# One core, a kernel of linear attention and a feed-forward layer: the store of the second weight's scales and their reload become two steps of the DMA queue, and the order of all steps is drawn anew

## What is computed

```python
x = x + attn(layernorm(x))     # attn: own norm, q,k,v = xn @ W (16 heads of 64), chunks of 128 rows
    # per head and chunk:  G = K.T @ K + 1e-4 I;  W = solve(G, K.T @ V)
    # U = I[:, :8]; twice: U = qr(W @ U).Q;  Wr = U @ (U.T @ W)
    # S = 0.9 * S + Wr;  out = 0.125 * (Q @ S);  attn = x + concat(out) @ Wo
x = x + ffn(layernorm(x))
    # bw = mean(|w|, axis=1) * sign(w) for w1 (1024 x 256) and w2 (256 x 1024)
    # out = gelu(x @ bw1.T + b1) @ bw2.T + b2
```

## Time and profile before

| what | value |
|---|---|
| median of 3 runs | 826.64 us (826.21 to 831.26) |
| the profiled execution | 823.01 us |
| its span, first to last instruction | 821.2 us |
| PE busy, share of the span | 756.2 us, 92% |
| DVE busy, share | 558.9 us, 68% |
| ACT busy, share | 483.2 us, 59% |
| POOL busy, share | 79.4 us, 10% |

### The profile page before, as it was taken

One profiled execution on the slowest core, in us unless ns is written; L12 is line 12 of the kernel. 1 busy time (PEld: TensorE's weight loads), 2 busy tenths in 40 slices (PEclk: granted clock), 3 DMA queues, 4 the chain that ended last, 5 costly groups with the idle time before them and its releaser, 6 DMA issues.

```text
span 821.2 us, 28518 instructions
## 1 busy us (share of the span) xinstructions
PE 756.2 (92%) x12336; PEld 494.7 (60%) x12336; DVE 558.9 (68%) x1530; ACT 483.2 (59%) x1000; POOL 79.4 (10%) x60
## 2 busy tenths in 40 slices
...
GB/s 257 294 28 87 138 73 58 154 132 164 50 110 161 139 100 91 139 101 152 89 116 102 196 160 125 150 98 97 90 195 59 168 74 59 86 86 77 54 26 26
DMA packets 262766, 93.63 MB, mean 114 GB/s; under 512 B 225008, under 2 KB 255984, under 8 KB 261616
## 3 DMA queue, kind: packets, MB, share of 16 engines
...
## 4 chain that ended last, share of the span: by engine, by line
PE 49%; DVE 23%; DMA 8%; issue 8%; ACT 5%; SPq 4%; POOL 1%; DVEq 0%; ACTq 0%; POOLq 0%
PE ring L1120 13%; DVE outer L936 8%; PE wide L1160 7%; DVE ax L945 6%; PE tok L1327 6%; PE ring L1138 3%; PE ring L1315 3%; PE wide L1247 3%; PE tok L1297 2%; PE small L1278 2%; PE sum L1288 2%; DMA ax<-lead_d 2%; DMA ax<-comp_d 2%; PE small L1168 2%; DVE rd L928 1%
## 5 line engine op out<-in xcount | busy, mean ns | idle before, releaser
L1120 PE MATMUL ring<-wkv,xt 128*128 128x512 f32 x512 | 245.0, 620 | 9.0 <-ACT rest L697 8.8
L936 DVE SCALAR_TENSOR_TENSOR outer<-ax,rd 128x448 f32<-128x448 f32 (+15 forms) x368 | 186.1, 533 | 8.8
L945 DVE TENSOR_TENSOR ax<-ax,outer 128x448 f32<-128x448 f32 (+15 forms) x368 | 163.2, 470 | 4.4
L1120 PEld LDWEIGHTS ring<-wkv,xt 128*128 128x128 f32 x512 | 93.4, 194 | 107.5 <-issue 90.0
L1327 PE MATMUL tok<-s2t,wkv 128*128 128x256 f16 x512 | 63.9, 282 | 8.3 <-DVE wkv L1045 7.5
L681 ACT COPY vals<-ring 128x512 f32<-128x512 f32 x64 | 37.3, 586 | 56.0 <-PE ring L1120 55.8
L577 POOL TENSOR_TENSOR root<-rdc,pos_half 128x32 f32<-128x32 f32 x8 | 43.4, 5428 | 266.6 <-DVE rdc L953 266.6
L1045 DVE TENSOR_TENSOR wkv<-ht,wkv 128x512 f16<-128x512 f32 x64 | 42.9, 688 | 37.9 <-ACT wkv L842 37.7
L1315 PE MATMUL ring<-y,s1t 128*128 128x512 f16 x256 | 61.8, 380 | 1.3 <-ACT ht L835 1.3
L1327 PEld LDWEIGHTS tok<-s2t,wkv 128*128 128x128 f16 x512 | 50.1, 101 | 20.0 <-DVE wkv L1045 10.7
L835 ACT ACTIVATE ht<-ring,b1c,alpha 128x512 f32<-128x512 f32 x64 | 48.9, 778 | 20.2 <-PE ring L1315 17.0
...
## 6 DMA issues: line engine op xcount, KB each, us to landing
...
xf<-inv_d SPq DMA_DIRECT2D x128, 32.0 KB, 2.1
```

Source lines behind the costliest of these rows:

```text
L936: at = note(V.scalar_tensor_tensor(out=t, in0=a[:, k, r0:r1].unsqueeze(2).broadcast_to([P, rows, cols]), scalar=r, in1=a[:, k, r0:HALF + k ...
L945: ends.append(note(V.tensor_tensor(rest, rest, t, ALU.subtract)))
L1120: ins = mm(dst[:], xt[:, g % 2, t, P * k:P * (k + 1)], weight[:, t, BANK * j:BANK * (j + 1)], start=t == 0, stop=t == KT - 1)
```

## The change

The step `al` is cut in two: `a1` stores the scales (after DVE has made them), `al` waits for the store and loads them back. In SP_ORDER `al` stood before `gs:7`; now `la:0`, the load of the first pass's lanes, stands first, then `cs:1 a1 cs:2 al`. At the same time all five tables are drawn anew. The steps in them are the same, apart from `a1`, and each does what it did: the instructions, their shapes and their number are unchanged. All lines below L378 move down by 2 in the new file.

```diff
-            def spread_alpha():
+            def store_alpha():
                 sp.wait_ge(alpha_done, 2)
                 load(alpha2_d.rearrange("(t p) -> p t", p=P), alpha2[:], allow_slow_non_contiguous=True).then_inc(alpha_stored, 16)
+
+            def spread_alpha():
                 sp.wait_ge(alpha_stored, 16)
                 load(alpha2r[:], alpha2_d.rearrange("(a d) -> a d", a=1).broadcast_to([P, DM])).then_inc(alpha_loaded, 16)
...
 SP_ORDER = """
-x:0 x:1 c w:0.0 w:0.1 w:1.0 w:1.1 zs wq wo b1 ff b2 rs:0 xs:0 xs:1 rs:1 gs:0 gs:1 x:2 x:3 gs:2 gs:3 gs:4 gs:5
-cs:0 rs:2 gs:6 x:4 al gs:7 cs:1 la:0 cs:2 xs:2 cs:3 rs:3 x:5 gs:8 cs:4 gs:9 gs:10 cs:5 gs:11 cs:6 xs:3 cs:7 rs:4
...
+x:0 c w:0.0 w:0.1 x:1 w:1.0 w:1.1 zs wq wo b1 ff b2 rs:0 xs:0 rs:1 gs:0 gs:1 xs:1 cs:0 x:2 x:3 gs:2 gs:3 gs:4
+gs:5 rs:2 gs:6 gs:7 x:4 la:0 cs:1 a1 cs:2 al xs:2 cs:3 rs:3 x:5 gs:8 gs:9 cs:4 gs:10 gs:11 cs:5 cs:6 xs:3 cs:7
...
```

More of the change, by code:

```diff
@@ L70 @@
+H:7.5 H:7.6 H:7.7 O:7.0 O:7.1
 """
 ACT_ORDER = """
-own norm:0 XT:0.0 XT:0.1 XT:1.0 XT:1.1 norm:1 K:0.0 K:0.1 K:1.0 K:1.1 K:2.0 G:0 K:2.1 G:1 K:3.0 K:3.1 K:4.0
-K:4.1 mag:0 K:5.0 K:5.1 K:6.0 mag:1 K:6.1 K:7.0 G:2 G:3 K:7.1 mag:2 V:0.0 V:0.1 G:4 G:5 C:0 V:1.0 norm:2 G:6
-V:1.1 WQ:0 mag:3 G:7 V:2.0 C:1 V:2.1 WQ:1 WQ:2 C:2 V:3.0 V:3.1 XT:2.0 XT:2.1 C:3 norm:3 K:8.0 K:8.1 K:9.0 K:9.1
-V:4.0 K:10.0 V:4.1 G:8 K:10.1 C:4 G:9 K:11.0 V:5.0 K:11.1 V:5.1 G:10 C:5 V:6.0 G:11 V:6.1 WQ:3 S2:0 C:6 V:7.0
-V:7.1 XT:3.0 XT:3.1 C:7 norm:4 K:12.0 K:12.1 K:13.0 K:13.1 G:12 K:14.0 G:13 K:14.1 K:15.0 K:15.1 T:0 G:14 G:15
@@ L103 @@
-hi:6.2 AU:30 AU:31 H:6.3 hi:6.3 H:6.4 H:6.5 hi:6.4 hi:6.5 H:6.6 H:6.7 hi:6.6 hi:6.7 n3:7 X3:7.0 X3:7.1 H:7.0
-H:7.1 hi:7.0 hi:7.1 H:7.2 H:7.3 hi:7.2 hi:7.3 H:7.4 H:7.5 hi:7.4 hi:7.5 H:7.6 H:7.7 hi:7.6 hi:7.7
+own norm:0 XT:0.0 XT:0.1 K:0.0 norm:1 K:0.1 K:1.0 K:1.1 K:2.0 G:0 K:2.1 G:1 K:3.0 K:3.1 V:0.0 V:0.1 XT:1.0
+XT:1.1 C:0 mag:0 K:4.0 K:4.1 K:5.0 G:2 G:3 K:5.1 K:6.0 mag:1 K:6.1 K:7.0 G:4 G:5 K:7.1 V:1.0 norm:2 G:6 G:7
+V:1.1 mag:2 C:1 mag:3 V:2.0 V:2.1 WQ:0 WQ:1 C:2 V:3.0 V:3.1 XT:2.0 XT:2.1 C:3 norm:3 K:8.0 K:8.1 K:9.0 K:9.1
@@ new lines @@
+K:10.0 V:4.0 G:8 K:10.1 V:4.1 G:9 K:11.0 C:4 K:11.1 V:5.0 V:5.1 G:10 G:11 V:6.0 C:5 V:6.1 WQ:2 WQ:3 C:6 V:7.0
+V:7.1 XT:3.0 XT:3.1 C:7 norm:4 K:12.0 K:12.1 K:13.0 K:13.1 G:12 K:14.0 G:13 K:14.1 K:15.0 T:0 K:15.1 G:14 G:15
+V:8.0 V:8.1 S2:0 C:8 V:9.0 V:9.1 S2:1 VS:0 C:9 ST:0 V:10.0 V:10.1 VS:1 C:10 V:11.0 VS:2 V:11.1 C:11 ST:1 V:12.0
+V:12.1 XT:4.0 VS:3 C:12 XT:4.1 norm:5 ST:2 V:13.0 V:13.1 K:16.0 C:13 V:14.0 V:14.1 ST:3 C:14 V:15.0 V:15.1
+XT:5.0 XT:5.1 C:15 norm:6 K:16.1 K:17.0 K:17.1 K:18.0 G:16 K:18.1 G:17 K:19.0 K:19.1 K:20.0 G:18 K:20.1 G:19
```

200 lines of the change are left out of this document (99 added, 101 removed).

## The result

The changed kernel takes 816.66 us (median of 4 runs, 813.62 to 820.63), the kernel before beside it 827.57 (826.21 to 831.26): ratio 0.9875, 95% interval 0.9843 to 0.9907. That is 10.3 us won, 7.7 to 13, where 21 were forecast. The profiled execution took 814.22 us against 823.01, so the pair of profiles differs by 8.8 us.

What follows compares the result with a forecast made beforehand. PE, busy 756.2 of 821.2 us, was taken as the bound, with 65 us of waits to win from. Gains of 9.5 + 10 + 1.5 = 21 us took the median from 826.6 to 805.6; range 795 to 819.

Steps and rivals of the forecast that it cites:

- Term 1: Start of pass 0: G:7's copy and store come earlier, lanes land at 76.1 instead of 86.24; 10 us, bounds 5.3 to 12.
- Term 2: PE until V:8.1: ACT's 8.26 us wait at T:0 shrinks to one or two, clock stays; 9.5 us, bounds 7 to 10.5.
- Carried through 160 to 350: Stretch where PE and DVE are nearly full: the head start is carried through and nothing is gained.
- Term 3: 350 to 440: DVE's waits there shrink or go, PE's at W:5 too; 10 us for both engines, bounds 0 and 13.
- PE can follow to about that: 350 to 440: PE, with 12.0 us of waits, can gain about DVE's 12.1 us.
- Term 4: Behind 440: late steps moved on DVE and PE cut waits of the same kind; 1.5 us, bounds -4 and +7.
- at other phases: Behind 440: the head start also meets the waits at other phases; part of the 1.5 us taken there.
- SyncE's queue would hold it up: Way to be wrong: SP, where a step like l2 is eight DMAs, becomes the one all wait for; no size.
- the head start alone: Rival: waits of 350 to 440 come back elsewhere, only 9.5 us stay, give or take 4: 817; chance 0.23.
- T copies holding ACT: Rival, slower: transposed copies earlier in ACT's list wait for DVE's scaling; three at full price give 836; chance 0.06.

Runs made afterwards that it cites:

- split_only: Kernel before with only SyncE's early piece new (gs:6 x:4 gs:7 la:0 cs:1 a1 cs:2 al xs:2): 823.93 us, ratio 0.9980.
- split_parked: Kernel before with only SyncE's order changed: a1 moved behind x:5, al behind cs:5, ahead of gs:11: 817.89 us, ratio 0.9899.
- split_far: Kernel before with only a1 and al moved on SyncE, a1 behind lx:1 and al behind cs:8 (near 155 us): 828.37 us, ratio 1.0001.
- after_far: Changed kernel with a1 moved behind lx:1 and al behind cs:8 on SyncE: 827.71 us, ratio 0.9988 against the kernel before.
- late_two: Changed kernel with T:6 on ACT behind hi:0.2 and X3:1.0, X3:1.1 on PE behind X1:8 O:0.0: 820.05 us, ratio 0.9911 against the kernel before.
- second_part: Kernel before's order for steps it had started by 150 us, the changed order for all later ones: 824.60 us, ratio 0.9967.

## Why the prediction was half right

**Term 1, 10 us: right.** 11.3, with two misses that nearly cancel: G:7's last copy ended at 65.71 (64.3 forecast), and its store landed in 1.6 us and not 4.70; the lanes took 7.1. split_only, split_parked and split_far give 8.3, 6.4 and 6.7 for the part that the split alone makes. That the wait for the scales costs nothing where the change puts it is right too: SyncE stood 4.7 us there. What I did not see is how much hangs on that place (after_far: 10 us), and that the lanes and the store beside cs:1 slow it: in the changed order that costs nothing, in the order before 5.5 us of PE. The trace decided rightly over the estimate from the Trainium skill, "DMA: Bandwidth & Descriptors", section "Anatomy of one DMA": the store took 7.6 us here and 8.0 in split_parked.

**Term 2, 9.5 us: right.** 9.4 at C:8, or 8.4 in work done. One step in it failed without effect: PE is not 2 us early at K:15.1 but level (0.2 late), as the wait before C:1, 5.03 us, is followed by the low clock (V:2.0 and V:2.1, 8 rows, take 4.24 us where 3.70 is usual). ACT does not wait at T:0 all the same.

**Carried through 160 to 350: nearly.** The lead went from 10.4 at F:0 to 8.5 at F:3, PE's waiting there from 3.1 to 4.9 us. PE's lead at 340 is 6.5 and 6.3.

**Term 3, 10 us for both engines: the place and sign right, the size 7 on DVE and 4 to 6 on PE. Here the prediction failed first.** B:5, ST:11 and B:6 wait no more, 10.1 of DVE's 14.0 us in the earlier trace rows, nor does PE at W:5; ZP:0 still does, longer than the 3.91 of the earlier trace rows:

```profile
421.23 0.42 DVE L996 TENSOR_TENSOR zm<-small,own 128x256 f32<-128x256 f32 x1 [5.79 <-PE small L1263]
```

DVE's waiting in the window fell from 19.3 to 12.2 us, and its lead rose by 7.2 from F:3 to F:6. The step that failed is "PE can follow to about that": PE's waiting in the window fell from 12.0 to 7.6, 4.4 us, and its lead rose by some 6 between 340 and 460.

**Term 4, +1.5, bounds -4 to +7: the second step that failed, in its sign.** PE's waiting went up, by 1.5 us from 440 to 600 (to 13.3, where the prediction's sign was 8 to 12) and by 1.0 behind it: -2.5, inside the bounds. By PE's lead it is about -3 from 460 to 700, by DVE's marks -4.5 from F:6 to the end, just outside them. I wrote that the head start meets the waits behind 440 "at other phases" and took a gain. What happened is that other waits came between 500 and 550, at LM:7 and X3:1.0 above all, and that the loss behind 500 comes with the redrawn middle, not with the head start. By PE's waiting terms 3 and 4 are 5.6 and 4.0 of the 10.7 us by which the sum was too high. That SyncE's queue would hold it up, which I named as a way to be wrong, is seen in late_two (sa:6 ahead of l1:8).

**The rivals.** The number, 817, is that of "the head start alone", and split_parked reaches nearly all of it with the head start only. Its mechanism is nearer to what happened than mine: of what the middle won on PE, about half was lost again in another place. It is not the whole of it, since second_part keeps 2.7 us (0.5 to 5.1) without any head start. T copies holding ACT cost nothing. The range, 795 to 819, holds the result, near its slow end.

**Open.** Why PE loses 5 to 8 us behind 500 when the middle is redrawn. Shown: it does so with either late order and with or without the head start, and late_two, which removed two of the waits there, put larger ones in their place. Not shown: which move of the middle makes them, and whether the late order of before is better by the 3 us that the times give.
